# Attention times V as fp32 products on 64-column halves of PE, in a transformer block on one core

## What is computed

```python
mod = jax.nn.swish(c) @ w_mod + b_mod
sh_msa, sc_msa, g_msa, sh_mlp, sc_mlp, g_mlp = jnp.split(mod, 6, axis=1)
xn = _ln(x) * (1 + sc_msa[:, None, :]) + sh_msa[:, None, :]
qkv = xn @ w_qkv + b_qkv
qkv = qkv.reshape(B, N, 3, NH, HD).transpose(2, 0, 3, 1, 4)
q, k, v = (qkv[0], qkv[1], qkv[2])
q = _ln(q, g_q)
k = _ln(k, g_k)
attn = jax.nn.softmax(jnp.einsum('bhqd,bhkd->bhqk', q, k) * HD ** (-0.5), axis=-1)
o = jnp.einsum('bhqk,bhkd->bhqd', attn, v)
o = o.transpose(0, 2, 1, 3).reshape(B, N, H) @ w_proj + b_proj
x = x + g_msa[:, None, :] * o
xn2 = _ln(x) * (1 + sc_mlp[:, None, :]) + sh_mlp[:, None, :]
h = jax.nn.gelu(xn2 @ w1 + b1, approximate=True)
x = x + g_mlp[:, None, :] * (h @ w2 + b2)
```

## Time and profile before

| | us |
|---|---|
| median of 3 runs | 2771.49 |
| lowest, highest | 2769.8, 2772.17 |
| span of the profiled execution | 2768.6 |
| PE busy in the span | 2734.0 |
| VectorE busy | 1990.4 |
| ScalarE busy | 1480.9 |
| GpSimd busy | 611.0 |

### The profile page before, as it was taken

The page is one execution under the profiler, slowest core; times in us unless marked ns, Lnnn a source line. Parts: engine busy times, 40 slices in busy tenths (PEclk is TensorE's granted clock), DMA queues, the critical chain, the costliest instruction groups (busy, mean ns, idle before and its releaser), DMA issues.

```text
span 2768.6 us, 41832 instructions
## 1 busy us (share of the span) xinstructions
PE 2734.0 (99%) x14674; PEld 1401.1 (51%) x14674; DVE 1990.4 (72%) x2803; ACT 1480.9 (53%) x2174; POOL 611.0 (22%) x420
## 2 busy tenths in 40 slices
PE   6999999999999999999999999999999999999999
PEld 3444444444444444444444444447566575756656
DVE  7899888899999888888888899953535334353421
ACT  4777777777777777777777777721111112111110
POOL 2552352224323222322332220200000000000000
PEclk9999999999999999999999999999999999999999
DMA  7512311223322122222222243041120202112000
GB/s 224 97 35 68 75 30 30 49 58 69 72 57 53 35 64 69 71 69 71 76 73 73 56 128 105 24 145 58 35 79 14 92 15 78 43 50 69 23 18 18
DMA packets 257261, 177.87 MB, mean 64 GB/s; under 512 B 172585, under 2 KB 210671, under 8 KB 256409
## 3 DMA queue, kind: packets, MB, share of 16 engines
q1 hardware_dynamic: 256826, 175.85, 24.0%
q10 hardware_dynamic: 288, 0.04, 0.0%
HBM read 96.23 MB, written 40.80 MB: 49 GB/s over the span
## 4 chain that ended last, share of the span: by engine, by line
PE 94%; DVE 3%; ACT 1%; SPq 1%; DMA 1%; issue 0%; POOL 0%; DVEq 0%; ACTq 0%
PE at_ps L1852 18%; PE at_ps L1201 16%; PE at_ps L1198 16%; PE at_ps L1189 16%; PE at_ps L1878 15%; PE at_ps L1220 10%; DVE at_plo L972 1%; PE at_ps L1871 1%; PE at_ps L1814 1%; PE at_ps L1831 1%; PE at_ps L1906 0%; DMA st_wm_first<-in_L_cond_b_mod 0%; PE at_ps L216 0%; SPq L475 0%; ACT at_aff L781 0%
## 5 line engine op out<-in xcount | busy, mean ns | idle before, releaser
L972 DVE TENSOR_TENSOR at_plo<-at_p 128x1024 fp32r<-128x1024 f32 x1024 | 1236.8, 1239 | 170.6 <-ACT at_p L751 167.0
L751 ACT ACTIVATE at_p<-at_ps 128x1024 f32<-128x1024 f32 x1024 | 1038.7, 1028 | 403.8 <-PE at_ps L1189 401.7
L1201 PE MATMUL at_ps<-at_plo,at_vr 128*37 128x512 f32 x2048 | 1072.1, 591 | 0.0
L1198 PE MATMUL at_ps<-at_p,at_v 128*73 128x512 bf16 x2048 | 796.5, 389 | 1.8 <-DVE at_plo L972 1.2
L620 POOL TENSOR_TENSOR at_tssq<-at_tssq,power 128x8 f32<-128x8 f32 x112 | 278.0, 2483 | 921.1 <-DVE at_tssq L915 920.5
L1852 PE MATMUL at_ps<-ml_w2s,ml_hid 128*128 128x288 f16 x3348 | 414.9, 286 | 0.0
L1878 PE MATMUL at_ps<-ml_xhi,ml_w 128*128 128x512 f16 x1296 | 381.9, 379 | 0.0
L1852 PEld LDWEIGHTS at_ps<-ml_w2s,ml_hid 128*128 128x128 f16 x3348 | 327.5, 98 | 82.0
L1198 PEld LDWEIGHTS at_ps<-at_p,at_v 128*73 128x73 f16 x2048 | 232.6, 114 | 247.4 <-DVE at_plo L972 9.0
L1201 PEld LDWEIGHTS at_ps<-at_plo,at_vr 128*37 128x37 f32 x2048 | 233.5, 114 | 220.6
L1189 PE MATMUL at_ps<-at_qk_even 109*128 (+1 forms) x1024 | 309.2, 383 | 4.9 <-ACT at_p L751 4.6
(11 more groups left out here) (189 smaller groups left out, 2226.6 us busy)
## 6 DMA issues: line engine op xcount, KB each, us to landing
head_sums<-at_oT SPq DMA_DIRECT2D x256, 72.0 KB
ml_held<-head_sums SPq DMA_DIRECT2D x64, 256.0 KB
at_xy<-in_L_cond_w SPq DMA_DIRECT2D x34, 288.0 KB
w_halves<-at_wq SPq DMA_DIRECT2D x68, 144.0 KB
at_xy<-in_x SPq DMA_DIRECT2D x32, 288.0 KB, 2.9
ml_x<-in_x SPq DMA_DIRECT2D x8, 1152.0 KB, 5.6
out<-ml_x SPq DMA_DIRECT2D x7, 1152.0 KB, 4.5
ml_held<-head_rden SPq DMA_DIRECT2D x24, 216.0 KB
```

The lines of the kernel that those rows point to most:

```text
L751: act.activation(p[:, s % NP, :], ps[:, 2 * (s % 2):2 * (s % 2) + 2, :].rearrange("p a n -> p (a n)"), ACT.Exp).then_inc(exp_done, 1)
L972: nc.vector.tensor_tensor(plo[:, s % NP, :], p[:, s % NP, :], high, ALU.subtract).then_inc(plo_ready, 1)
L1198: nc.tensor.matmul(acc[0:VW, bass.ds((U % 2) * CH, CH)], v16[:, h % 2, 2 * s + a, 0:VW], high, start=(s == 0 and a == 0), stop=False, skip ...
L1201: last = nc.tensor.matmul(acc[0:RW, bass.ds((U % 2) * CH, CH)], vr[:, h % 2, 2 * s + a, 0:RW], plo[:, s % NP, a * CH:(a + 1) * CH], start= ...
```

## The change

- `sums`: the two products per key tile, and `plo`, `v16`, `vr` and GpSimd's `head`, are gone. The first key tile of a step is multiplied as plain fp32 with 37 columns (v and a column of ones, now kept in `v32` itself) into partitions 0 to 36 of the bank, the second into partitions 64 to 100, so the two use different column halves of PE.
- `scores`: each product of 128 columns becomes two of 64, on the two column halves.
- `tile_products`: whole 128 columns, as before.
- `keep_sums` on VectorE takes the place of ScalarE's `keep_oT`: a copy of partitions 64 to 100 to `half`, then an addition of partitions 0 to 36 into `oT`. It stands in step 3. SP stores two DMAs per unit instead of three; behind attention `add_o` and its loads are gone.
- PE's program is written out for all groups. In a group's last unit ScalarE's copy of v moves from step 2 to step 4.
- Buffers move by 512 bytes; the new tensors are as below.

```diff
-        v32 = sb("v32", [P, 2 * NT, GH, HD], F32, 108288)
+        v32 = sb("v32", [P, 2 * NT, GH, RW], F32, 108288)
...
-        plo = sb("plo", [P, NP, 2 * CH], F32R, 175872)
...
-        v16 = sb("v16", [P, 2, NT, VP], F16, 192256)
-        vr = sb("vr", [P, 2, NT, RP], F32R, 196992)
-        oT = sb("oT", [VW, CH], F32, 201856)
+        half = sb("half", [RW, CH], F32, 196992)
+        oT = sb("oT", [RW, CH], F32, 201856)
...
+            def keep_sums(U):
+
+                bank = bass.ds(((U + 1) % 2) * CH, CH)
+                dve.wait_ge(pv_done, U * STEPS + 1)
+                dve.wait_ge(oT_ready, U - 1 + OT)
+                nc.vector.tensor_copy(half[:, :], acc[HP:HP + RW, bank]).then_inc(half_ready, 1)
+                dve.wait_ge(half_ready, U)
+                dve.wait_ge(oT_stored, (U + 1) * OS)
+                nc.vector.tensor_tensor(oT[:, :], acc[0:RW, bank], half[:, :], ALU.add).then_inc(oT_ready, 1)
...
                     dve.wait_ge(exp_done, n + 3)
-                    high = p[:, s % NP, :].bitcast(BF16).rearrange("p (n t) -> p n t", t=2)[:, :, 1]
-
-                    nc.vector.tensor_tensor(plo[:, s % NP, :], p[:, s % NP, :], high, ALU.subtract).then_inc(plo_ready, 1)
+                    if s == LAG and not first:
+                        keep_sums(U)
...
                 pe.wait_ge(exp_done, U * STEPS + s + 1)
                 qk = qkT[G % 2]
                 for a in range(2):
-                    last = nc.tensor.matmul(ps[:, 2 * (s % 2) + a, :], qk[0:SW, GH + h, (2 * s + a) * P:(2 * s + a + 1) * P],
-                                            qk[0:SW, h, bass.ds(qc * CH, CH)], start=True, stop=True)
+                    for c in range(0, P, HP):
+                        key = (2 * s + a) * P + c
+                        last = nc.tensor.matmul(ps[c:c + HP, 2 * (s % 2) + a, :], qk[0:SW, GH + h, key:key + HP],
+                                                qk[0:SW, h, qc * CH:(qc + 1) * CH], start=True, stop=True)
                 last.then_inc(scores_ready, 1)

-            def sums(U, h, s):
-
-                pe.wait_ge(plo_ready, U * STEPS + s + 1)
+            def sums(G, U, h, s):
+
+                pe.wait_ge(exp_done, U * STEPS + s + 3)
+                bank = slice((U % 2) * CH, (U % 2 + 1) * CH)
                 for a in range(2):
-                    high = p[:, s % NP, a * CH:(a + 1) * CH].bitcast(BF16).rearrange("p (n t) -> p n t", t=2)[:, :, 1]
-                    nc.tensor.matmul(acc[0:VW, bass.ds((U % 2) * CH, CH)],
-                                     v16[:, h % 2, 2 * s + a, 0:VW], high,
-                                     start=(s == 0 and a == 0), stop=False, skip_group_check=True)
-                    last = nc.tensor.matmul(acc[0:RW, bass.ds((U % 2) * CH, CH)],
-                                            vr[:, h % 2, 2 * s + a, 0:RW],
-                                            plo[:, s % NP, a * CH:(a + 1) * CH],
-                                            start=False, stop=(s == STEPS - 1 and a == 1), skip_group_check=True)
+                    last = nc.tensor.matmul(acc[a * HP:a * HP + RW, bank], v32[:, (G % 2) * NT + 2 * s + a, h, :], p[:, s % NP, a * CH:(a + 1) * CH],
+                                            start=(s == 0), stop=(s == STEPS - 1))
                 last.then_inc(pv_done, 1)
```

More of the change, by code:

```diff
@@ L419, in attention_mlp @@
         tq_stored = [sem(f"tq_stored{n}") for n in range(len(STORED))]
[L420 to L421 removed]
+        scores_ready, exp_done, pv_done = sem("scores"), sem("exp"), sem("pv")
+        half_ready, oT_ready, oT_stored = sem("half"), sem("oT"), sem("oT_stored")
         t_mm, t_sq, t_ssq, t_msq, t_rstd, t_yn, t_yg, t_high, t_low, t_stored = (
@@ L588, in _ @@
         def _(pool):
[L589 to L613, removed]
             def tile_power(X):
@@ L691, in _ @@
                     rest.gpsimd_early(pool, u)
-                if u % NCH == 2 and U // NCH + 1 < B * NH:
-                    head(U // NCH + 1)
             rest.gpsimd(pool)
@@ L743, in unit @@
                     n = U * STEPS + s
-                    if s == LAG and not first:
-                        keep_oT(U)
                     act.wait_ge(scores_ready, n + 1)
@@ L1328, in attend @@
                     if s >= LAG:
-                        sums(U, h, s - LAG)
-                    elif not first:
-                        sums(U - 1, (h - 1) % GH if fixed and qc == 0 else h, s - LAG + STEPS)
-                    if fresh and s < 2 and not first:
+                        sums(G, U, h, s - LAG)
+                    elif U:
+                        sums((U - 1) // UNITS, U - 1, (U - 1) % UNITS // NCH, s - LAG + STEPS)
+                    if fresh and s < 2 and U:
                         tile_products(U + 1, 0 if at_end else u + 1, G + (2 if at_end else 1), range(7 * s, 7 * s + 7))
-                    if G == GROUPS - 1 and fixed:
+                    if G == GROUPS - 1:
                         rest.tensor_early(pe, u, s)
@@ L1460, in __init__ @@
         sides = lambda k: (0,) if k < KF else (0, KT)
-        loads = [len(sides(k)) * (2 + len(list(head_rows(k)))) for k in range(KC)]
+        loads = [len(sides(k)) * (1 + len(list(head_rows(k)))) for k in range(KC)]
         self.sides = sides
@@ L1495, in load_sums @@
             for side in self.sides(k):
-                for part in range(2):
-                    sp.dma_start(self.slot[side:side + rows, k % 2, part, :],
-                                 self.sums_dram[part, J:J + 1, k * P:k * P + rows, :].rearrange("c d t -> (c d) t")).then_inc(loaded, 16)
+                sp.dma_start(self.slot[side:side + rows, k % 2, 0, :],
+                             self.sums_dram[J:J + 1, k * P:k * P + rows, :].rearrange("c d t -> (c d) t")).then_inc(loaded, 16)
                 for p0, p1, h, heads in head_rows(k):
```

132 lines of the change are left out of this document (49 added, 83 removed).

## The result

| | before | after |
|---|---|---|
| median of the runs beside each other | 2771.0 us (2769.8 to 2772.17) | 2750.8 us (2748.89 to 2751.06) |
| span of the profiled execution | 2768.6 us | 2748.7 us |
| busy: PE, VectorE, ScalarE, GpSimd | 2734, 1990, 1481, 611 us | 2718, 953, 1430, 304 us |

The ratio of the changed kernel to the one before is 0.9926, 95% interval 0.9912 to 0.9940: 20.2 us less by the medians, 19.9 us by the profiled spans. Forecast were 2757 us and 14 us less.

What follows compares the result with a forecast made beforehand. PE's own instruction stream was taken as the bound (busy 2734 of 2768.6 us). Terms -62.5 + 52.3 - 4 = -14.2 us took 2771.5 to 2757 us; range 2740 to 2793 us.

Steps and rivals of the forecast that it cites:

- PV as fp32 on halves: Attention sums: two fp32 products side by side on PE's halves take 0.862 us a step, against 0.93 for four products.
- Scores on halves: Attention scores: each pair of 64-column products takes 0.22 us; new step 1.302 instead of 1.363 us, -62.5 us in all.
- The change of tiling: Around QKV chunks, projection chunks and transposes on whole columns: 249 round trips of 0.21 us, +52.3 us.
- Waits for plo: PE's waits in attention for VectorE's `plo` vanish: -4 us, bounds 0 and -6.
- VectorE's copy and addition: Per attention unit, out of PSUM: some 1.2 us on VectorE against 9.9 removed, beside PE's work.
- the new waits: VectorE's copy waits for the previous unit's last sums, its addition for SP's store: costs nothing.
- the written-out program: PE's instructions for all groups written out instead of looped: costs nothing, steps being equally long either way.
- The border between fp16 and fp32: Rival, each attention step: passing from 16-bit to 32-bit products costs 0.033 us, +34 us, 2791 us; chance 0.28.
- the 0.033 us of the old pair: Old PV products: bf16 plus fp32r takes 0.033 us more than two plain products, ascribed to strided bf16 reading or fp32r.
- Late exponentials: Rival: shorter steps make PE wait some 0.1 us in each of 110 units, +11 us, 2768 us; chance 0.10.
- Halves overlap in fp16: Denies the rival that 64-column score halves don't overlap: scores 0.87 us a step, some 3200 us; chance 0.04.
- Free changes of tiling: Rival: changing tiling costs nothing for column halves, around whole-column chunks, giving 2705 us; chance 0.06.

Runs made afterwards that it cites:

- 220 fewer: Changed kernel with each attention QKV product issued as two of 64 columns, one on each half of PE: 2701.0 us, 0.9755 of the kernel before.
- 110 fewer: Changed kernel with a unit's 14 QKV products in one chunk behind step 1 instead of two chunks of 7: 2723.9 us.
- 775 more: Changed kernel with scores as two products of 128 columns again, PV staying on halves: 2927.3 us.

## Why the prediction was right, step by step

**PV as fp32 on halves: right.** 0.862 us for both tiles was forecast from line 216, 0.86 measured. That they run side by side is shown by the run on the same half, +0.858 us a step.

**Scores on halves: right in kind, a little too dear.** I took 0.22 us a pair between ends of 0.216 and 0.43; a pair takes 0.215 to 0.219, two of them 0.434, which is the lower end. The 0.22 came from 0.54 us in the earlier trace rows, split by assumption into 0.10 for the change and two pairs; 2 x 0.216 and 0.11 would have fitted it as well. New step 1.294 instead of 1.302: -70.4 instead of -62.5 us, the largest miss, 8 us.

**The change of tiling: right, 0.01 too cheap.** 0.21 us a round trip was forecast, 0.22 to 0.225 measured; the counts (220, 24, 5) were right. The part left out is the first pair of scores behind a chunk, 0.02 longer. Five transposes cost 0.29 each rather than 0.21. Together +56.3 instead of +52.3 us. The forecast had called itself wrong outside 0.20 to 0.22: the price stands at that edge or just over it. Three runs confirm it with other counts: 220 fewer (-50 us, 0.226 each), 110 fewer (-27, 0.245), 775 more (+176.5, 0.228). By unit lengths, which are free of the scattering start, they give 0.22, 0.23 and 0.23. That tiling explains all of it, and not the neighbourhood of fp32 and fp16, is shown by the QKV products on halves: the same fp32 and fp16 neighbours, and no surcharge.

**Waits for plo: the term was mis-sized.** -4 us with bounds 0 and -6; the traces have -6.75 and the kernel before without the subtraction -7.4. I had taken the odd units at sight and a guess for the rest; summing all 126 units against the usual length of their kind gives the number directly, and would have been possible before.

**VectorE's copy and addition, ScalarE, the new waits, the written-out program: nothing, as forecast.** Copy and addition take 0.693 and 0.683 us (1.38 a unit, forecast 1.2), and units exceed their usual lengths by 0.2 us in all. Writing PE's program out is 0.6 us in an experiment of its own, inside its interval. What stands between the forecast's -14.2 and -19.9 is thus 8 for the scores and 3 for the stalls, less 4 for the round trips and 1 for the later start. That the total is off by no more than 6 us owes something to misses of opposite sign.

**The rivals.** The border between fp16 and fp32 does not exist here: a step is 1.294 us, no more than 6 x 0.216. I had ascribed the 0.033 us of the old pair to "that pair (a strided bf16 read, or fp32r)". The stride is out (3 to 4 ns), and a border inside the pair isn't needed: two fp32r products without one take as long. What holds is that fp32r with 37 columns takes 0.233 us on its own, 0.017 of the 0.033; whether by its type or by its narrow weights, and where the rest of the 0.033 comes from, no run tells. Late exponentials did not come: the answer to the earlier trace rows in the changed kernel is

```profile
1623.26 1.02 ACT L702 ACTIVATE at_p<-at_ps 128x1024 f32<-128x1024 f32 x1 [0.27 <-PE at_ps L1151]
```

Its scores began at 1622.62, so its buffer is wanted two steps later, at 1625.21, 0.93 us after its end (0.94 forecast), and PE waits for ScalarE 2.5 us in 3 times. Halves overlap in fp16: 0.215 to 0.219 a pair. The rule that I had put beside that rival, from the Trainium skill, "TensorE: Matmul & The Clock Gate", Part 3, has loads overlap only when the row group differs; here the row group is the same, the columns differ, and nothing of a load shows, neither in 0.215 us nor in pairs of 0.12. Free changes of tiling are refuted by 0.22 us.

**What I did not see.** The forecast named the QKV products on whole columns as what "eats the gain", and did not ask what they would cost on halves. By its own numbers, 249 x 0.21 = 52 us lay there, more than three times the change it forecast; the two edits that put these products on halves took 56 us.

## What to carry to other kernels

PE has a state, its tiling, and each change of it between neighbouring products cost about 0.1 us here: count the changes in the instruction order, not the products. If one product of an inner loop moves to halves, everything that stands between its repetitions should move too, or be gathered in one place. Two fp16 products of 64 columns side by side cost no more than one of 128, at 512, 432 and 288 moving columns, so staying in the mode was free; fewer moving columns were not tried.

Where one engine's instruction stream was the bound, distances from start to start gave the forecast; only the stalls needed more. And a floor taken from another shape is a guess: 0.216 us holds for weights of 128 columns, not for narrow 16-bit ones on the whole of PE.

## What the runs showed of the hardware

- A round trip from 64-column halves to 128 columns and back costs 0.22 to 0.23 us, in three pieces: 0.10 at the entry, 0.10 at the exit, 0.02 on the first pair behind it. It is the same with 7 or with 14 products between (0.22 and 0.23 by unit lengths). Transposes with load records of 0.14 us pay 0.27 to 0.29.
- Two 16-bit products in a row on whole columns with weights of 73 and 37 columns take 0.32 to 0.35 us each; with weights of 128 columns, the same for all four products of a step, 0.222. With fp32r behind each the pair takes 0.46. On halves, weights of 64 columns hide even in 0.12 us.
- In the kernel with both tiles on the lower half, a score product and an fp32 product begin at the same 2408.05 in PE's timeline, which they never do in the changed kernel. The lower half has fp32 products without a pause (starts 0.43 us apart), so the score product must be one of the upper half: a product on a free half did not wait for a pending one on the other. That is worked out from the starts; the trace doesn't name the half, and it is one run.

```profile
2407.62 0.40 PE L1151 MATMUL at_ps<-at_qk_odd 109*64 109x512 f16 x1
2408.05 0.59 PE L1160 MATMUL at_ps<-at_p,at_v 128*37 128x512 f32 x1
2408.05 0.40 PE L1151 MATMUL at_ps<-at_qk_odd 109*64 109x512 f16 x1
```
